# Conditioned top-2 mixture of experts on one core: logits computed ahead of y, routing interleaved with y's rows, and y's split spread over three engines

## The reference

```
ys = cond / 16
d  = rsqrt((ys*ys) @ (weight*weight) + 1e-8)
y  = ((x * ys) @ weight) * d                       # (2, 1024, 256)
lang   = softmax(y @ lang_w.T + lang_b)            # 4 languages
router = softmax(y @ router_w.T + router_b + 0.1 * (lang[idx] + lang_padded[idx + 1]))   # 8 experts
top_p, top_i = top_k(router, 2);  top_p /= sum(top_p)
expert_out[e] = gelu(y @ w1[e] + b1[e]) @ w2[e] + b2[e]      # 256 -> 1024 -> 256, fp32
out = x + sum over the two picked experts of top_p * expert_out
```

## Time and profile before

| | us |
|---|---|
| median of 3 runs | 298.55 |
| lowest and highest | 296.48, 300.69 |
| the profiled execution | 297.96 |
| its span, first to last instruction | 296.2 |
| TensorE busy in the span | 272.3 (92%) |
| VectorE, ScalarE, GpSimd busy | 189.2, 195.7, 179.4 |

### The profile page before, as it was taken

How to read it: one execution, slowest core, us unless ns; L and a number is a source line. 1 busy time by engine, 2 the same in 40 slices (tenths; PEclk the granted TensorE clock), 3 DMA queues, 4 the chain that set the end, 5 groups by cost and what they waited for, 6 DMA issues and landing times.

```text
span 296.2 us, 8964 instructions
## 1 busy us (share of the span) xinstructions
PE 272.3 (92%) x3066; PEld 223.1 (75%) x3066; DVE 189.2 (64%) x427; ACT 195.7 (66%) x426; POOL 179.4 (61%) x161
## 2 busy tenths in 40 slices
PE   8999988689999999999999999999999999999800
PEld 6878967588889998777777777777787878778400
DVE  1857788799699788565565565555655656556410
ACT  3356469599697898757767677677676676775500
POOL 8200056884666598676878577777767776464230
PEclk9999999979999999999999999999999999999975
DMA  6899996399874333465574644853544434323130
GB/s 145 325 400 388 353 348 206 109 314 460 306 191 90 56 57 72 56 101 65 76 91 77 87 70 78 76 91 64 83 77 74 75 74 76 51 39 38 20 35 0
DMA packets 39497, 39.93 MB, mean 135 GB/s; under 512 B 19504, under 2 KB 35328, under 8 KB 39296
## 3 DMA queue, kind: packets, MB, share of 16 engines
q1 hardware_dynamic: 31872, 28.89, 32.8%
q0 software_dynamic: 7552, 10.45, 23.0%
q10 hardware_dynamic: 32, 0.01, 0.0%
HBM read 27.61 MB, written 9.64 MB: 126 GB/s over the span
## 4 chain that ended last, share of the span: by engine, by line
PE 82%; DMA 5%; DVE 4%; issue 3%; ACT 2%; POOL 1%; POOLq 0%; DVEq 0%
PE ps L643 33%; PE ps L660 30%; PE ps L539 5%; PE ps L652 4%; PE ps L557 4%; DMA rows<-y_rows,idx 3%; DMA out<-onehot,idx 3%; PE ps L481 1%; PE ps L620 1%; DVE wsp L951 1%; PE ps L512 1%; PE ps L521 1%; ACT wsp L781 1%; PE ps L497 1%; POOL out L470 1%
## 5 line engine op out<-in xcount | busy, mean ns | idle before, releaser
L643 PEld LDWEIGHTS ps<-onehot,wsp 128*128 (+1 forms) x1872 | 130.7, 99 | 34.4 <-issue 1.1
L643 PE MATMUL ps<-onehot,wsp 128*128 128x128 f16 x1872 | 154.2, 220 | 0.8 <-ACT onehot L811 0.6
L827 ACT ACTIVATE pay<-ps,cur 128x128 f32<-128x128 f32 x312 | 117.4, 459 | 51.7 <-issue 37.9
L660 PE MATMUL ps<-wsp,pay 128*128 (+1 forms) x616 | 138.1, 316 | 1.2 <-DVE pay L1113 1.2
L470 POOL DMA_INDIRECT out<-onehot,idx x39 | 67.8, 1739 | 33.7 <-DMA out<-onehot,idx 15.3
L1113 DVE SCALAR_TENSOR_TENSOR pay<-pay,cur 128x512 f16<-128x512 f32 x72 | 54.9, 762 | 29.2 <-ACT pay L815 27.9
L439 POOL DMA_INDIRECT rows<-y_rows,idx x39 | 57.0, 1463 | 17.9 <-issue 11.0
L461 POOL TENSOR_SCALAR onehot<-onehot,cur 128x256 f32<-128x256 f32 x36 | 38.1, 1059 | 24.0 <-DVE onehot L1131 15.8
L660 PEld LDWEIGHTS ps<-wsp,pay 128*128 128x128 f16 x616 | 45.7, 97 | 6.9 <-issue 1.7
L1107 DVE TENSOR_SCALAR pay<-pay,cur 128x512 f16<-128x512 f32 x36 | 18.8, 521 | 26.0 <-ACT pay L827 26.0
L815 ACT ACTIVATE pay<-pay,cur 128x512 f16<-128x512 f32 x36 | 26.0, 722 | 1.2
(11 more groups left out here) (176 smaller groups left out, 195.5 us busy)
## 6 DMA issues: line engine op xcount, KB each, us to landing
stage<-in_L_ffn_w SPq DMA_DIRECT2D x9, 1024.0 KB, 10.6
wsp<-in_L_ffn_w SPq DMA_DIRECT2D x7, 1024.0 KB, 12.0
y_rows<-pay SPq DMA_DIRECT2D x4, 512.0 KB, 9.3
wsp<-in_x SPq DMA_DIRECT2D x3, 512.0 KB, 7.9
b2bc<-in_L_ffn_b SPq DMA_DIRECT2D x1, 1024.0 KB, 4.8
rows<-y_rows,idx POOLq DMA_INDIRECT x39
out<-onehot,idx POOLq DMA_INDIRECT x39, 4.1
wsp<-in_x SPq DMA_DIRECT2D x2, 256.0 KB, 5.5
```

Source lines behind the costliest of these rows:

```text
L643: last = mm(ps[:, HB + (2 * j + g) % RING, c * P:(c + 1) * P], wsp[:, bass.ds(e, 1), o:o + P].rearrange("p a f -> p (a f)"), xsp[:, j % RI ...
L660: last = mm(ps[:, OB + j % 2, 0:width], hsp[:, (2 * j + g) % NH, part, c, :], wsp[:, bass.ds(e, 1), o + w:o + w + width].rearrange("p a f ...
L827: last = a.activation(to, ps[:, HB + (2 * j + g) % RING, c * P:(c + 1) * P], ACT.Gelu, bias=cur[:, j % CURS, cc:cc + 1], scale=cur[:, j % ...
```

## The change

1. **Logits first.** `rows_of_y` computes only the 256 columns of y. A new `logits(t)` computes the 12 logits of all 16 tiles into one bank first, with the last four transpositions of x among them; VectorE adds the bias to all in one instruction. Then y's rows follow, through three banks (0, 1, 3) in place of five.
2. **Routing beside y.** VectorE starts routing when the logits are there; the low parts of the odd rows are put between its steps (`ROWS_AT`, `low_rows`), the counts, ranks and mapping stand among y's rows on TensorE. The bound for y's scale is computed after the logits' bias.
3. **Even rows.** For an even row ScalarE writes the high part and the scaled value in fp32 (`whole`, three buffers); GpSimd subtracts the high part (`low_even`). TensorE may write row t when row t - 3 is read: by ScalarE's second activation (`y_full`) for an even, by VectorE (`y_low`) for an odd one.
4. **Grams** of groups 0 to 3 move: before, 0 and 1 after y, 2 after the ranks, 3 after the mapping; now 0 among y's last rows and 1, 2, 3 after the mapping, group 2 in bank 3. The 19 matmuls of `keep_warm` there are dropped. GpSimd's scales for groups 1 and 2 stand between its first gathers.
5. **ScalarE's weights.** Before the first tile it splits halves 0 and 2 in place of 0, 2, 4, 6, 9; 4 and 6 stand around the first tile's first gelus, 9 at the head of the next list.
6. **Expert numbers** are loaded 8 at a time in place of 31, TensorE's first before the first transposition of gathered rows in place of after two tiles' up blocks.
7. **SP and the end.** The routing weights are written by SP, behind y's second quarter. ScalarE weighs tile 36 before, not after, the first gelus of the last tile.

The core of the diff:

```diff
-HIGHS = {0: (0, 2, 4, 6, 9), 1: (8, 3), 2: (7,), 3: (11,), 5: (1, 10), 7: (12,), 9: (13,), 11: (14,), 13: (15,), 15: (5,)}
+HIGHS = {0: (0, 2, 4, 6), 1: (9, 8, 3), 2: (7,), 3: (11,), 5: (1, 10), 7: (12,), 9: (13,), 11: (14,), 13: (15,), 15: (5,)}
...
-GRAM_BANKS = (7, 5, 6, 7, 5, 7, 5)
+GRAM_BANKS = (7, 5, 3, 7, 5, 7, 5)
...
-BANKS_Y = 5
-WIDTH_Y = D + NR
+Y_BANKS = (0, 1, 3)
+ROWS_AT = {"in": (1,), "best": (3,), "second": (5,), "picked": (7,), "slots": (9,), "tiles": (11,), "half": (13,), "hot": (15,)}
...
-BATCH = 31
+BATCH = 8
...
+        def low_of_y(engine, t):
+            return engine.scalar_tensor_tensor(out=y_halves[:, t, 1, :], in0=ps[:, Y_BANKS[t % 3], 0:D], scalar=yscale[:, 0:1],
+                                               in1=y_halves[:, t, 0, :], op0=ALU.mult, op1=ALU.subtract)
...
             for c in range(4):
-                sp.wait_ge(y_split, 4 * c + 4)
+                sp.wait_ge(y_low, 2 * c + 2)
+                sp.wait_ge(y_low_even, 2 * c + 2)
...
                 if c == 1:
                     load_weights(9)
+                    sp.wait_ge(p_ready, 1)
+                    for b in range(NB):
+                        sp.dma_start(y_tiles[:, b, :, D:ROW], payv[:, b * TB:(b + 1) * TB, D:ROW]).then_inc(p_written, 16)
             load_weights(3)
             load_weights(7)
...
+            def low_even(t):
+                pool.wait_ge(y_full, t // 2 + 1)
+                g.tensor_tensor(y_halves[:, t, 1, :], whole[:, t // 2 % 3, :], y_halves[:, t, 0, :], ALU.subtract).then_inc(y_low_even, 1)
+
+            low_even(0)
+            low_even(2)
+            pool.wait_ge(best, 1)
...
+            low_even(10)
+            low_even(12)
+            scale_early(0)
+            low_even(14)
...
             for j in range(ROWS):
                 gather(j)
+                if j == 2:
+                    scale_early(1)
+                if j == 3:
+                    scale_early(2)
...
+            def logits(t):
+                pe.wait_ge(xt_ready, t // 2 + 1)
+                for k in range(KD):
+                    last = mm(ps[:, LB, t * NR:(t + 1) * NR], xT[:, t, k * P:(k + 1) * P], Wyr[:, t // TB, k, D:],
+                              start=(k == 0), stop=(k == KD - 1))
+                return last
+
             def rows_of_y(t):
-                pe.wait_ge(xt_ready, t // 2 + 1)
-                if t >= BANKS_Y:
-                    pe.wait_ge(lg_read, t - BANKS_Y + 1)
+                if t >= 3:
+                    if t % 2:
+                        pe.wait_ge(y_full, (t - 3) // 2 + 1)
+                    else:
+                        pe.wait_ge(y_low, (t - 3) // 2 + 1)
...
-            keep_warm(5, 1, 512)
...
-            keep_warm(4, 1, 512)
...
-            keep_warm(WARM, 1, 512)
...
+            pe.wait_ge(te_ready, 1)
+            expert(E)
             transpose_rows(0)
             blocks((0, 0), None)
             transpose_rows(1)
             blocks((0, 1), None)
             sum_squares(3)
-            pe.wait_ge(te_ready, 1)
-            expert(E)
...
+            def high_of_y(t):
                 act.wait_ge(y_psum, t + 1)
-                a.activation(y_halves[:, t, 0, :], ps[:, t % BANKS_Y, 0:D], ACT.Copy, scale=yscale[:, 0:1]).then_inc(y_high, 1)
...
+                a.activation(y_halves[:, t, 0, :], ps[:, Y_BANKS[t % 3], 0:D], ACT.Copy, scale=yscale[:, 0:1]).then_inc(y_high, 1)
+                if t % 2 == 0:
+                    if t >= 6:
+                        act.wait_ge(y_low_even, t // 2 - 2)
+                    a.activation(whole[:, t // 2 % 3, :], ps[:, Y_BANKS[t % 3], 0:D], ACT.Copy, scale=yscale[:, 0:1]).then_inc(y_full, 1)
...
             copy_x(0)
+            copy_sums(2)
             copy_x(1)
+            split_high(4)
             gelus(0, 0)
+            split_high(6)
             for j in range(NT):
-                if j == NT - 1:
-                    weigh(NT - 3)
                 gelus(j, 1)
...
                 for n in HIGHS.get(2 * j + 1, ()):
                     split_high(n)
+                if j == NT - 2:
+                    weigh(NT - 3)
                 if j + 1 < NT:
                     gelus(j + 1, 0)
...
+            def low_rows(name):
+                for t in ROWS_AT[name]:
+                    dve.wait_ge(y_high, t + 1)
+                    low_of_y(v, t).then_inc(y_low, 1)
+
```

161 lines of the change are left out of this document (86 added, 75 removed).

## The result

The changed kernel takes 319.93 us (median of four executions, 315.94 to 320.49), the kernel before 298.62 beside it on the same chip. The ratio is 1.0695, with a 95% interval of 1.0634 to 1.0756: 21 us slower, where 3 were forecast. The range ended at 306.

The account below looks back on a forecast made before the run. TensorE, busy for 211.73 of 212 us from 60 to 272 us, was taken as the bound, leaving the start to decide. 297.96 + 1.2 (tile start) + 1.4 (ScalarE) + 1.7 (clock) + 0.4 (loads) - 1.4 (tail) = 301.3 us; range 294.5 to 306.

Parts of the forecast that it names:

- The pace of the logits: At the start on TensorE: 64 narrow logits records at 0.12 us each, 7.6 us, all logits done at 23.7.
- The rival for dearer logits: Logits at 0.17 a record, halfway to the 0.23 of y's 268 columns: +3.2, 304.5 us; chance 2%.
- Rows of y and routing: Between logits and mapping: from logits at 23.7, indices at 48.1 and y's last quarter issued at 46.2.
- the rival by which they hold up y: GpSimd's slow even low parts and y's landing delay the first gather, everything waits for y in memory: 305.9 us; chance 15%.
- routing beside y: VectorE's routing steps run among y's rows, so indices come at 48.1 instead of 49.72, 1.6 us sooner.
- the mutual waiting: During y's rows, TensorE and VectorE wait for each other in turn through three banks, so indices come near 48.
- From y's last quarter to the first tile: Quarter issued 46.2, weights of halves 3 and 7 landed 54.0, gather 3.4 from issue; tile start 55.2, +1.2.
- ScalarE's backlog: After the first tile: late high parts delay gelus to 17.5 after it; TensorE waits 3.7, block ends at 20.8: +1.4.
- The 13.8 for when TensorE would be there: TensorE reaches the block of tiles 2 and 1 13.8 us after the tile start, at full clock.
- The 1.7 for the clock behind the wait: After TensorE's wait for ScalarE, a slow clock costs 1.7 us again; bounds 0 and 1.7.
- Register loads: Loads of 8 expert numbers take 0.7 us each, mostly hidden by TensorE's queue: +0.4 in all.
- The tail: At the end: tile 36's scatter can be issued at 274.99, 4.58 after the one before, not 276.39: -1.4.

Follow-up runs that it names:

- run 8: The changed kernel again, without an edit: 318.0 us median, four executions at 314.84, 315.08, 320.92 and 322.21.
- run 10: Changed kernel with y's first three rows placed among the logits, behind those of tiles 2, 6 and 10: 314.75 us median, ratio 1.0479.
- run 2: Kernel before with 32 narrow matmuls (12 columns, 64 records, result unread) ahead of y's rows: 312.39 us median, ratio 1.048.
- run 4: Kernel before with only the weighing of tile 36 moved ahead of the last tile's first gelus: 297.94 against 298.08 us, ratio 0.998.
- run 12: Kernel before with ScalarE's high parts of halves 4, 6 and 9 made as late as in the changed kernel: 300.46 against 298.32 us, ratio 1.0059.
- run 6: Changed kernel with GpSimd's scales of group 0 behind its last even low part, not before it: 318.19 us median, ratio 1.0715.
- run 11: Changed kernel with even rows' low parts back on VectorE, without ScalarE's second activation and GpSimd's subtractions: 319.12 us median, ratio 1.0649.
- run 1: Changed kernel with a 512-column matmul, result unread, behind each of the 16 pairs of logits matmuls: 325.46 us median, the profiled execution 311.33.
- run 7: Changed kernel with weight halves 3 and 7 loaded after the first gather, their gram, maximum and scale moved later: 312.98 us median, ratio 1.0541.
- run 5: Kernel before with expert numbers loaded 8 at a time in place of 31: 297.12 against 297.78 us, ratio 1.000.
- run 13: Kernel before with TensorE's load of 31 expert numbers ahead of the first tile, 6 fillers for 10, tile 36 weighed earlier: 296.17 against 297.79 us, ratio 0.993.
- run 3: Changed kernel with ScalarE's high parts of halves 4 and 6 made ahead of the first tile: 310.31 us median, ratio 1.0332.
- run 9: Changed kernel with halves 3 and 7 loaded after the first gather and high parts of 4 and 6 before the first tile: 317.96 us median, ratio 1.0682.
- run 14: Changed kernel with y rows among logits, late loads of halves 3 and 7, half 4 split early, one load of 31 numbers: 318.62 us median.

## Why the prediction was wrong

**The pace of the logits.** The step that failed first reads "64 x 0.12 us ... = 7.6 us. I take that price since both are bound by the same fp32 weight load, not by columns". The price is right at the full pace (0.12 in runs 8 and 10), but TensorE ran these matmuls at the lower pace: 0.21, logits over at 31.6 and not 23.7, +7.9. Run 2 shows it by itself. The prediction had read the granted clock behind the idleness of the earlier trace rows and did not ask what it would be at the start, where both kernels are at the lower pace at 11 us, and where the change puts 20 us of narrow matmuls in the place of the rows of y behind which, in runs 4 and 12, the pace was back. The rival for dearer logits, at 0.17 a record, was the right place with half the size and a chance of 2%.

**Rows of y and routing.** From the logits to the issue of y's last quarter it is 25.9 us, not 22.5, +3.4: y's first three rows at the lower pace (4.8 in place of 2.8), and 2.07 of waits of TensorE for low parts where 0.9 was counted. That the two engines wait for each other was right. GpSimd's low parts were priced at 0.9 and took 0.67 to 0.96; the rival by which they hold up y is wrong (runs 6 and 11). Whether routing beside y would gain its 1.6 at the full pace no run shows by itself. In run 1 the indices come at 51.0, but behind 16 fillers of 0.22 us; less these, by my estimate, it is 47.5, near the 48.1 of the forecast. So the mutual waiting was added up about right, and it was the start under it that moved.

**From y's last quarter to the first tile** it is 13.4 us, not 9.0, +4.4. "Behind it 2 MB of weights ... with 1.2 for the landing 54.0" put the weights in 7.8 after that issue; the second waited for was there after 11.4 (57.50 to 68.85), at 314 GB/s where the sum had 380. They also slowed the gather, which was given 3.4 as before and took 6.8. Run 7 takes both away and has 9.8 from mapping to first tile. 7.9 + 3.4 + 4.4 make the 15.7.

**ScalarE's backlog** was right in mechanism, and alone in the kernel before it ends the block at 20.6 for 20.8 (run 12). That the wait came out as 3.38 for 3.7 is partly luck. The 13.8 for when TensorE would be there doesn't follow from its rows: 70.2 - 54.04, less 1.76 and 1.7, is 12.7, and run 5 has 12.4; the wait would have been near 4.8. In the changed kernel the first up blocks run at the lower pace (2.72), behind the waits for the loads, so TensorE was there at 15.4 and the gelus at 18.6, for 17.5. This makes most of the 23.9 in place of 22.5. The 1.7 for the clock behind the wait came (the block takes 5.1 in place of 3.3, granted clock 0.67), but the argument for it, that a longer idleness than today's 1.76 must cost as much, doesn't hold: behind 2.69 in run 12 and behind 1.76 in run 4 the clock stays at 1.00, and the matmuls take what they take at the full pace.

**Register loads.** "If a load's time goes by its numbers, eight take ... 0.7 us": they take 0.70 in the median, 0.60 to 1.08:

```profile
L306 PEldq TENSOR_LOAD <-te x4: 599/703/1081, 68.9 to 259.8; - x4
```

But "the three inside the stream cost about nothing", on which +0.4 rested, failed: they cost 1.6 (0.40, 0.39 and 0.82 us of idleness), +1.7 in the loop; the lead of TensorE's queue hides less than 0.7. The Trainium skill (DMA: Bandwidth & Descriptors, Latency and other measured facts) has a floor of about 600 ns for such a load; the shortest here, 0.60, agrees. The idleness ahead of tile 2 was the load's, as held (runs 5 and 13).

**The tail** gave 1.5 for 1.4 in the table, but by two things: the scatter of tile 36 is issued 5.07 behind the one before it, where it was 5.98 and 4.6 was forecast, so the edit gave 0.9, and that earlier scatter stood 0.5 sooner against the gelus that the table counts from. By the time alone it can't be told from nothing (run 4).

```profile
292.95 1.58 POOL L494 DMA_INDIRECT out<-onehot,idx  x1 [0.93 <-DMA out<-onehot,idx]
298.02 1.57 POOL L494 DMA_INDIRECT out<-onehot,idx  x1 [3.48 <-DMA out<-onehot,idx]
```

What stays open is what decides at 11 to 13 us. In every profile the eight transpositions at 9.4 to 9.5 us take 1.77 to 2.08, where eight at the full pace take 1.09 (at 20 us in the kernel before). Some executions are back at the full pace by 13 (the kernel before, runs 1, 3, 5, 7, 8, 9, 10 and 13), some aren't (the changed kernel, runs 2, 4, 6, 11, 12 and 14), and of those that are, some fall again among the logits, at 16 (runs 7 and 9), 18 (run 8) or 21 us (run 3). The code up to the logits is the same in all versions of the changed kernel, and the times at which x arrives differ by a microsecond or two. That a stretch of narrow matmuls keeps TensorE there is shown (run 2); what lets it come back at 12 us, or not, isn't. How much of run 3's median is its edit and how much the start is open too; its span behind the first tile says 5.0.

## What to carry to other kernels

Before wide matmuls are moved back to let narrow ones go first, price the narrow ones, and all that follows until the wide ones have run a while, at TensorE's lower pace as well: here it cost 8 us, five times the 1.6 that the new order was to win. A load that is "issued last" belongs in the sum twice, once for who waits for it and once for the small transfer, such as the first gather, that shares the queue with it. Cures found one by one are to be run together before they are believed: two of them here cancelled each other by a scale that GpSimd makes late, and a load that was free where TensorE waited for a gather (run 13) cost 2.47 us where it didn't (run 14).

## What the runs showed of the hardware

- TensorE's pace at the start differs between executions of one program: 8 logit records took 0.96 until 18 us in one profile (an execution of 314.84) and 1.72 from 14 us on in another (319.40). In the kernel before it moves less: its first tile starts at 53.7 to 54.4 us where the pace is back by 13, and at 56.5 where it is back by 18 (runs 4 and 12).
- The record of the granted clock can miss it. In runs 2 and 14 it reads 1.00 while records of 12 columns take 0.21 us and, in run 14, a row of y 2.05, and in runs 4 and 12 while two rows of y take 3.3 us in place of 2.04. The Trainium skill (TensorE: Matmul & The Clock Gate, Part 1) warns that such records have been seen to be unreliable; these four traces agree. Durations of one known form are the surer clock.
- A GpSimd step of 128 x 3 numbers took 1.86 and 2.32 us beside VectorE's 2.35 us low parts, and ended with them, where such a step took 0.19 to 0.40 in the changed kernel (run 9). The prediction had 0.640 as the worst.
